# Expert stages of a sorted mixture-of-experts layer: the last LayerNorm's shift and scale on ScalarE, its gain and residual as two wide VectorE operations one tile later

## What is computed

```python
x = x + 0.5 * ffn(layernorm(x))
x = x + retention(layernorm(x))
x = x + 0.5 * ffn(layernorm(x))

def ffn(src):
    x = LN1(src + attention(src))                 # 16 heads of 8
    keys = (x @ router_w + router_b)[..., 0]
    expert = remainder(floor(keys), 4)            # one expert per token
    y = relu(x @ W1[expert] + b1[expert]) @ W2[expert] + b2[expert]   # 128 -> 512 -> 128
    return LN2(x + y)                             # LN: (x - mean) / sqrt(var + 1e-5) * gamma + beta
```

## Time and profile before

| what | us |
|---|---|
| median of 3 runs | 1122.56 (1122.55 to 1128.83) |
| the profiled execution | 1117.45 |
| its span, first to last instruction | 1115.1 |
| busy in the span: TensorE / VectorE / ScalarE / GpSimd | 900.9 / 778.1 / 654.2 / 621.8 |
| expert stages | about 334 to 430 and 1017 to 1115 |

### The profile page before, as it was taken

The page is one execution under the profiler, slowest core; times in us unless marked ns, Lnnn a source line. Parts: engine busy times, 40 slices in busy tenths (PEclk is TensorE's granted clock), DMA queues, the critical chain, the costliest instruction groups (busy, mean ns, idle before and its releaser), DMA issues. The chain is left out here.

```text
span 1115.1 us, 26787 instructions
## 1 busy us (share of the span) xinstructions
PE 900.9 (81%) x8603; PEld 664.7 (60%) x8603; DVE 778.1 (70%) x1930; ACT 654.2 (59%) x1326; POOL 621.8 (56%) x921
## 2 busy tenths in 40 slices
PE   3898999999828882888888885699999999964984
PEld 2565666666518872566566664466666666644883
DVE  2887888888835884365565553368888888853886
ACT  1587888888815451243443342279888888852552
POOL 3144765766553664376766665224665765653675
PEclk9999999999968996799999997579999999986998
DMA  9884990000018753000000000000000000005771
GB/s 304 358 338 56 367 395 22 19 9 19 21 39 256 214 175 84 1 1 1 0 0 0 0 1 0 1 1 2 21 14 14 19 10 19 20 20 173 218 237 55
DMA packets 41556, 97.67 MB, mean 88 GB/s; under 512 B 5224, under 2 KB 24958, under 8 KB 36876
## 3 DMA queue, kind: packets, MB, share of 16 engines
q1 hardware_dynamic: 35980, 84.16, 23.4%
q0 software_dynamic: 5504, 12.63, 3.2%
HBM read 44.68 MB, written 53.13 MB: 88 GB/s over the span
## 5 line engine op out<-in xcount | busy, mean ns | idle before, releaser
L1165 DVE TENSOR_REDUCE mx<-duo 128x4 fp32r<-128x1024 f32 x256 | 312.4, 1220 | 75.5 <-PE duo L520 70.2
L906 ACT ACTIVATE probs<-duo 128x1024 f32<-128x1024 f32 x256 | 263.2, 1028 | 56.0 <-PE duo L526 51.7
L520 PE MATMUL duo<-stacks 32*128 32x256 f32 x1024 | 133.8, 339 | 32.4 <-DVE mx L1165 24.3
L573 PE MATMUL duo<-probs,v_st 128*32 128x256 f32 x2048 | 141.1, 394 | 0.0
L1365 DVE TENSOR_TENSOR ret<-duo,dm 128x768 f32<-128x768 f32 x64 | 61.2, 957 | 105.5 <-PE duo L754 101.7
L526 PE MATMUL duo<-q_st,stacks 32*128 32x256 f32 x1024 | 130.9, 334 | 4.7 <-ACT probs L906 4.7
L520 PEld LDWEIGHTS duo<-stacks 32*128 32x128 f32 x1024 | 80.9, 192 | 67.8 <-issue 27.1
L513 PE MATMUL duo<-qk_hi,sel_r 128*128 128x256 f32 x256 | 83.7, 347 | 9.4 <-DVE qk_lo L1154 9.1
L1480 POOL TENSOR_TENSOR a_ln<-mv_ln,eps_ln 128x2 f32<-128x2 f32 x32 | 6.3, 196 | 150.9 <-DVE mv_ln L1132 150.9
L654 PE MATMUL duo<-w,probs 128*128 x608 | 77.0, 280 | 7.7 <-issue 4.4
L526 PEld LDWEIGHTS duo<-q_st,stacks 32*128 32x128 f32 x1024 | 77.6, 187 | 6.1 <-issue 3.2
(11 more groups left out here) (208 smaller groups left out, 2410.6 us busy)
## 6 DMA issues: line engine op xcount, KB each, us to landing
x_sorted<-ret SPq DMA_DIRECT2D x2, 17476.0 KB, 49.0
wbuf<-w_pack SPq DMA_DIRECT2D x38, 512.0 KB
ret<-x_sorted SPq DMA_DIRECT2D x22, 257.0 KB
stacks<-x_sorted SPq DMA_DIRECT2D x12, 257.0 KB
wside<-w_pack SPq DMA_DIRECT2D x38, 66.0 KB
w_pack<-wbuf SPq DMA_DIRECT2D x2, 1024.0 KB, 7.2
decay_rows<-prow SPq DMA_DIRECT2D x1, 1536.0 KB
probs<-x_sorted SPq DMA_DIRECT2D x4, 257.0 KB
```

What stands on the lines that cost most here:

```text
L520: return pe.matmul(score_bank[h % 2][:, t * SEQ:(t + 1) * SEQ], q_st[r:r + 32, g, t * P:(t + 1) * P], k_st[r:r + 32, g, :], start=True, st ...
L573: last = pe.matmul(pv_bank[32 * j:32 * j + 32, cols], v_st[:, t, h, :], probs[:, h % RING, t, :], start=(t == 0), stop=(t == TT - 1))
L906: act.activation(probs[:, h % RING:h % RING + 2, :, :], prob_duo[:].rearrange("p (n t q) -> p n t q", n=2, t=TT), ACT.Exp, scale=SCALE).th ...
L1165: dve.tensor_reduce(rows, score_duo[:].rearrange("p (n t k) -> p n t k", n=2, t=TT), AX.X, ALU.max, negate=True).then_inc(max_done, 1)
```

## The change

LN2's normalisation is written as z * unit + drop with unit = rstd and drop = -mean * rstd. VectorE computes `drop` in a fourth small operation. ScalarE applies both, per half, in `normal(k - 2)`, placed after `relu(k)`. VectorE's `finish` is split: `moments(k - 2)` (the four small operations) stays where `finish` was, and the new `finish(k - 3)` behind it works one tile later, on both halves at once: times gamma in place, then plus the residual. The loop gets one more turn. `deliver` waits for one signal per tile in place of two. `unit` and `drop` have two buffers.

```diff
@@ -272,6 +272,8 @@
               [ret_flat[:, n * TT * ROW:(n + 1) * TT * ROW] for n in range(5)] + [probs_flat[:, 2048:2048 + TT * ROW]]
               + [stacks[:, n * TT * ROW:(n + 1) * TT * ROW].bitcast(FP32) for n in range(3)]]
         blank = ret_flat[:, 0:8 * ROW]
+        drop = sb("drop", [P, 2, TT])
+        unit = sb("unit", [P, 2, TT])
         six_r = sb("six_r", [P, TT, 6])
         mv_r = sb("mv_r", [P, TT, 2])
         x_sorted = [nc.dram_tensor(f"x_sorted{n}", (ROWS, ROW), FP32, kind="Internal").ap() for n in range(2)]
@@ -937,6 +939,14 @@
                         act.activation(hid[:, n % 2, c, :], bank[c][:, 0:SEQ], ACT.Relu,
                                        bias=wside[:, n % 3, c:c + 1]).then_inc(h_ready, 1)
 
+                def normal(k):
+                    n = first + k
+                    act.wait_ge(ln2, n * 8 + 8)
+                    wait(act, yo_ready, n - 1)
+                    for t in range(TT):
+                        last = act.activation(zn[:, n % 2, t, :], z[:, n % 3, t, :], ACT.Identity, bias=drop[:, n % 2, t:t + 1], scale=unit[:, n % 2, t:t + 1])
+                    last.then_inc(zn_ready, 1)
+
                 for k in range(-1, TILES + 2):
                     if k + 1 < TILES:
                         round_x(k + 1)
@@ -944,6 +954,8 @@
                         seeds(first + k - 2, "ln2")
                     if 0 <= k < TILES:
                         relu(k)
+                    if k >= 2:
+                        normal(k - 2)
 
             def phase(base):
                 def body(i):
@@ -1139,11 +1151,13 @@
                     dve.wait_ge(seed[which], b * 2 + 2)
                     dve.scalar_tensor_tensor(s["a"][:], s["mv"][:, :, 1], LN_EPS, s["seed"][:], ALU.add, ALU.mult).then_inc(done, 1)
                     return
-                dve.wait_ge(done, b * 9 + 4 + part)
+                dve.wait_ge(done, b * 8 + 4 + part)
                 if part == 1:
                     dve.scalar_tensor_tensor(s["c"][:], s["a"][:], -0.5, s["seed"][:], ALU.mult, ALU.mult).then_inc(done, 1)
                 elif part == 2:
-                    dve.scalar_tensor_tensor(s["rstd"][:], s["c"][:], 1.5, s["seed"][:], ALU.add, ALU.mult).then_inc(done, 1)
+                    dve.scalar_tensor_tensor(unit[:, b % 2, :], s["c"][:], 1.5, s["seed"][:], ALU.add, ALU.mult).then_inc(done, 1)
+                elif part == 3:
+                    dve.scalar_tensor_tensor(drop[:, b % 2, :], s["mv"][:, :, 0], -1.0, unit[:, b % 2, :], ALU.mult, ALU.mult).then_inc(done, 1)
 
             def split_qk(b):
 
@@ -1266,28 +1280,29 @@
                     dve.tensor_tensor(z[:, n % 3], bank[4 + n % 2][:, 0:SEQ].rearrange("p (t d) -> p t d", t=TT), xb[:, n % 3], ALU.add).then_inc(z_ready, 1)
                     dve.wait_ge(z_ready, n + 1)
                     layer_norm(n, "ln2", lambda t: z[:, n % 3, t, :], None)
-                    dve.wait_ge(ln2, n * 9 + 2)
+                    dve.wait_ge(ln2, n * 8 + 2)
                     layer_norm_moments(n, "ln2")
+
+                def moments(k):
+                    n = first + k
+                    for part in range(4):
+                        layer_norm_end(n, "ln2", part)
 
                 def finish(k):
                     n = first + k
-                    s = ln_scratch["ln2"]
-                    for part in range(3):
-                        layer_norm_end(n, "ln2", part)
-                    dve.wait_ge(ln2, n * 9 + 7)
-                    for t in range(TT):
-                        dve.scalar_tensor_tensor(zn[:, n % 2, t, :], z[:, n % 3, t, :], s["mv"][:, t, 0:1], g2_b, ALU.subtract, ALU.mult).then_inc(ln2, 1)
+                    dve.wait_ge(zn_ready, n + 1)
+                    dve.tensor_tensor(zn[:, n % 2], zn[:, n % 2], g2_b.unsqueeze(1).to_broadcast([P, TT, P]), ALU.mult).then_inc(zg_ready, 1)
                     wait(dve, yo_out[n % 3], 32 * (n // 3))
-                    for t in range(TT):
-                        dve.wait_ge(ln2, n * 9 + 8 + t)
-                        dve.scalar_tensor_tensor(yo[:, n % 3, t, :], zn[:, n % 2, t, :], s["rstd"][:, t:t + 1], xt[n % XT_RING][:, t, DM:2 * DM],
-                                                 ALU.mult, ALU.add).then_inc(yo_ready, 1)
-
-                for k in range(-1, TILES + 2):
+                    dve.wait_ge(zg_ready, n + 1)
+                    dve.tensor_tensor(yo[:, n % 3], zn[:, n % 2], xt[n % XT_RING][:, :, DM:2 * DM], ALU.add).then_inc(yo_ready, 1)
+
+                for k in range(-1, TILES + 3):
                     if k + 1 < TILES:
                         split_x(k + 1)
-                    if k >= 2:
-                        finish(k - 2)
+                    if 2 <= k < TILES + 2:
+                        moments(k - 2)
+                    if k >= 3:
+                        finish(k - 3)
                     if 1 <= k <= TILES:
                         add_ffn(k - 1)
 
@@ -1570,7 +1585,7 @@
 
                 def deliver(k):
                     n = first + k
-                    pool.wait_ge(yo_ready, n * 2 + 2)
+                    pool.wait_ge(yo_ready, n + 1)
                     beat()
                     home = x_mid if ph == 0 else A["out"].rearrange("b s d -> (b s) d")
                     for t in range(TT):
```

More of the change, by code:

```diff
@@ L215, in build @@
         xb = probs_flat[:, 3072:3840].rearrange("p (n t d) -> p n t d", n=3, t=TT)
-        z, zn, zg, yo = token_bufs[:, 0:3], token_bufs[:, 3:5], token_bufs[:, 5], token_bufs[:, 6:9]
+        z, zn, yo = token_bufs[:, 0:3], token_bufs[:, 3:5], token_bufs[:, 6:9]
         x_hi = sb("x_hi", [P, 2, SEQ], FP32R)
@@ L328, in build @@
         xT_ps, xhi_ready, xlo_ready, xb_ready = sem("xT_ps"), sem("xhi_ready"), sem("xlo_ready"), sem("xb_ready")
-        up_ps, h_ready, down_ps, z_ready, zg_ready, yo_ready = sem("up_ps"), sem("h_ready"), sem("down_ps"), sem("z_ready"), sem("zg_ready"), sem("yo_ready")
+        up_ps, h_ready, down_ps, z_ready, zn_ready, zg_ready, yo_ready = sem("up_ps"), sem("h_ready"), sem("down_ps"), sem("z_ready"), sem("zn_ready"), sem("zg_ready"), sem("yo_ready")
         rln, gn, set_bv, rsum_ready = sem("rln"), sem("gn"), sem("set_bv"), sem("rsum_ready")
@@ L861, in seeds @@
                 s = ln_scratch[which]
-                act.wait_ge(ln_sem[which], b * 9 + 4)
+                act.wait_ge(ln_sem[which], b * 8 + 4)
                 act.activation(s["lnv"][:], s["mv"][:, :, 1], ACT.Ln, bias=eps_col[:]).then_inc(seed[which], 1)
```

## The result

The changed kernel takes 1136.7 us (median of 10 runs, 1132.1 to 1141.9) against 1123.33 for the kernel of before (10 runs, 1120.58 to 1128.83). The ratio is 1.011, 95% interval 1.0083 to 1.0137: about 12 us slower. The profiled execution took 1134.76 us. The two expert stages, from the first transposes to the end of the last scatter, take 100.79 and 102.40 us where they took 95.36 and 94.65, +13.2 us together.

A forecast was written before the change was run, and what follows sets the result against it. VectorE's collision with GpSimd's add of b2 bounds the kernel; the load chain comes next. Sixteen periods at 4.54 give +1.6 and +2.5 us, ends 2 x 2.6: 1122.56 + 9.3 = 1131.9, shaded to 1131; range 1118 to 1138.

The forecast's parts named there:

- the load chain: Y, GpSimd's scatters and add of b2, SP's weight and x loads, TensorE, next Y: 4.42 to 4.61 us per tile.
- rival A: VectorE/GpSimd collision loop and load chain meet, wide operations come late: period 4.7 us, 1137 us in all, chance 0.25.
- part 3: VectorE against GpSimd's add of b2: both wide operations get stuck, a loop of 4.52 to 4.62 us per tile.
- Part 4: Later Y makes the load chain span four periods, not five: 17.69 to 18.44 us, 4.42 to 4.61 per tile.
- Y: End of a tile's last operation on VectorE, which triggers GpSimd's scatters of that tile.
- x leg: From SP's weight load until TensorE gets the x loaded behind those weights: 5.24 to 5.99 us.
- short collisions: A few tiles' collision of VectorE with GpSimd would cost 0.3 us less each; forecast shaded from 1131.9 to 1131.
- Part 6: End of each expert stage: last scatter over at A + 7.4, where A starts the last tile's small operations; +2.6 us, twice.
- Part 5: ScalarE's two added operations, 0.6 to 0.94 us per tile, cost nothing because ScalarE idles 2.27 us per tile.
- B: First wide operation always slips in, or only L1569's own row is closed; loads decide: period 4.15, 1119 us, chance 0.12.
- C: Load chain has more in hand than counted and the collision is gone: period 3.8 us, 1108 us, chance 0.08.

The follow-up runs named there:

- the tiny add: GpSimd's add of x and b2 cut to one element: on the kernel of before 0.9794, on the changed kernel 1.0021 of before.
- the lag alone: Kernel of before with its four narrow VectorE operations one tile later, nothing moved to ScalarE: 1.0114 of before.
- one period more in the chain: Changed kernel with GpSimd's add of b2 placed one tile further ahead, before the delivery of finished tiles: 0.9987 of before.
- lag_both: Kernel of before with narrow operations one tile later, finish ahead of the small operations, and add of b2 one tile further ahead: 0.9839 of before.
- after_both: Changed kernel with VectorE's finish ahead of the small operations and GpSimd's add of b2 one tile further ahead: 0.9831 of before.

## Why the prediction was right

The time and its sign came out, and so did the main step, the load chain. Three things limit that. The measured 1136.7 is near the upper end of the range of 1118 to 1138 and is the number of rival A (1137, chance 0.25), 5.7 us above my own 1131. The collision loop of part 3 was not there as drawn. And the second chain was not seen. That the period of 4.54, taken from part 3, lies so near the measured mean is in part luck.

- *The bound.* That VectorE's 4.5 us are 3.48 of work and a collision with GpSimd's add of b2 is shown by the tiny add: 3.47 where it is gone. It holds for the tiles with a collision; 11 of the 38 tiles of the kernel of before have both L1279 free.
- *Part 3, VectorE's free work hardly changes (3.42 for 3.48).* Held: the fast periods at the start of a stage are 3.43, before 3.47. The collision did not stay where I put it. I had both wide operations stuck in nearly every tile, as a loop of 4.52 to 4.62; both are stuck in 7 tiles, at least one in 16, and in 16 tiles a small operation is, because VectorE comes late by amounts that change from tile to tile. My sign for it (wide operations of 0.9 us or more beside the add of b2) came in 15 tiles.
- *Part 4, the load chain over four periods.* This was the main step and it held in kind: its waits appeared, the lag alone gives them and the whole slowdown, and one period more in the chain takes most of them away. In size: forecast 17.69 to 18.44, measured 19.04. The term that was mis-sized is the last one, from the add to Y, 3.50 against 4.60. It was summed from VectorE's free work, but the collision (0.67 per period) and the wait for the late x_hi (0.33) fall into it. The first is rival A's meeting of the two loops, in the small operations as much as in the wide ones, though A's condition, an x leg of 5.99 or more in most tiles, did not come: its mean is 5.52. The second is the chain through x_lo, which closes over three periods. The other legs together are 14.44, within the 14.19 to 14.94 of the forecast.
- *The period.* 4.54 was taken for 16 of 18; (80.40 - 6.86) / 16 = 4.60 and (81.80 - 6.86) / 16 = 4.68 were measured, +2.5 and +4.8 per stage in place of +1.6 and +2.5. Against my 79.4 us per stage that is 1.0 and 2.4 more, 3.4 of the 5.7 us between 1131 and 1136.7. The rest is 0.8 for the kernel of before, whose median was higher in this measurement, 0.9 that I took off for short collisions, and 0.6 from the first transposes to the first adds.
- *Part 6, the ends.* +2.6 us each was forecast, 9.25 - 6.61 = 2.64 and 9.26 - 6.64 = 2.62 were measured.
- *Part 5, ScalarE at nothing.* Right as to its effect: no instruction waited for L947 in the trace of the changed kernel, and `lag_both` is level with `after_both`. One operation is outside of its bounds of 0.30 to 0.47 (0.50), the pair inside of 0.6 to 0.94 (0.88): see the last section.
- *Rivals B and C* fell: a mean period of 4.1 or less came in the changed kernel only once the chain had its fifth period back.

## What to carry to other kernels

Before an operation goes one turn of the loop later, follow its signal through every in-order queue behind it, not only to its reader. Here Y's reader (the scatter) had time, but the add of b2 stood behind the scatter, and the weight load behind that add. Follow every way that the load takes back to the signal: here two of them, over four and over three periods, were equally tight. Issuing the operation that a future load needs one tile sooner, ahead of the wait for finished work, cost nothing here: moving that one line gave back what the change took, and with the delayed work placed in another wait as well the kernel came to 0.983 of before.

## What the runs showed of the hardware that was not expected

ScalarE's operation with per-partition scale and bias, 128x128 from SBUF, is dearer than my upper bound of 0.47 for one (the group, then one pair in the timeline):

```profile
L947 ACT ACTIVATE token_bufs<-token_bufs,drop,unit x76: 477/499/508, 348.9 to 1123.2; 128x128 f32<-128x128 f32 x76
```
```profile
1102.25 0.88 ACT L947 ACTIVATE token_bufs<-token_bufs,drop,unit 128x128 f32<-128x128 f32 x2 [0.26 <-DVE drop L1160]
```

0.50 us for 128 columns, where a ReLU of 256 columns from PSUM with a bias alone takes 0.47. Two back to back take 0.88 together.

Operations of two columns are held as those of 128 or 256 are: with two inputs in SBUF, 0.16 us becomes 0.59 and 0.63 beside GpSimd's indirect DMA and add, and up to 0.78 in other tiles. The first one runs while the row of the indirect DMA does (1100.06 to 1101.04) and ends 0.12 us after it (1101.16), as if that row's second half were closed too. With the add of b2 cut to one element nothing is held beside the same indirect DMAs. Why it is closed there, and only where a full add follows, no run here tells.
